# Eight gather buffers instead of four, and the returned rows added in steps of five behind the first late tile's sum

## What is computed

```python
x = x + xattn(layernorm(x), ctx)
h = layernorm(x)
shared_out = expert(h, shared_up[0], shared_down[0])
probs = softmax(h @ router_w)                   # 8 experts
top_k_prob, top_k_idx = top_k(probs, 2)         # two per row
routed_out = sum_e gates[..., e] * expert(h, routed_up[e], routed_down[e])
return shared_out + routed_out + x              # expert: gelu(h @ up) @ down
```

## Time and profile before

| | us |
|---|---|
| median of 3 runs | 2279.95 |
| lowest, highest | 2277.34, 2282.57 |
| the profiled execution, its own time | 2280.16 |
| its span, first to last instruction | 2278.4 |
| outside the span | 1.76 |
| TensorE busy | 2210.9 (97%) |
| VectorE busy | 1804.1 (79%) |

### The profile page before, as it was taken

How to read it: one execution, slowest core, us unless ns; L and a number is a source line. 1 busy time by engine, 2 the same in 40 slices (tenths; PEclk the granted TensorE clock), 3 DMA queues, 4 the chain that set the end, 5 groups by cost and what they waited for, 6 DMA issues and landing times. The chain is left out here.

```text
span 2278.4 us, 40701 instructions
## 1 busy us (share of the span) xinstructions
PE 2210.9 (97%) x13782; PEld 1571.2 (69%) x13782; DVE 1804.1 (79%) x2424; ACT 1370.5 (60%) x2035; POOL 270.1 (12%) x300
## 2 busy tenths in 40 slices
PE   5999999999999999999999999999997999999997
PEld 4656666665666666566566666655886999999996
DVE  6898889899899988989988997898533555557776
ACT  5676566567567666756756765564433555567762
POOL 1100000000001000000000010001472111122210
PEclk8999999999999999999999999999998999999998
DMA  6336236334433522542452362223563434446656
GB/s 238 87 102 187 72 88 185 96 95 126 137 93 105 181 78 84 157 129 75 118 161 85 102 188 78 68 69 123 183 226 121 130 123 136 129 140 218 219 196 225
DMA packets 149277, 305.01 MB, mean 134 GB/s; under 512 B 34784, under 2 KB 71776, under 8 KB 146080
## 3 DMA queue, kind: packets, MB, share of 16 engines
q1 hardware_dynamic: 138688, 272.46, 38.9%
q0 software_dynamic: 10176, 30.45, 3.7%
q10 hardware_dynamic: 288, 0.26, 0.0%
HBM read 189.31 MB, written 79.20 MB: 118 GB/s over the span
## 5 line engine op out<-in xcount | busy, mean ns | idle before, releaser
L927 ACT ACTIVATE probs<-scores 128x1024 f32<-128x1024 f32 x512 | 504.3, 1024 | 212.3 <-PE scores L742 116.4
L1206 DVE TENSOR_TENSOR sums<-sums,probs 128x1024 f32<-128x1024 f32 x384 | 470.4, 1225 | 14.3 <-DVE sums L1206 0.5
L795 PE MATMUL sum_ps<-probs,v_nat 128*64 128x512 f32 x2056 | 469.8, 599 | 1.1 <-DVE probs L1099 1.1
L742 PE MATMUL scores<-q_split,k_split 64*128 64x512 f32 x3072 | 427.2, 409 | 1.6 <-issue 1.5
L1099 DVE TENSOR_SCALAR probs<-probs 128x2048 f32<-128x2048 f32 x256 | 312.9, 1222 | 144.6 <-ACT probs L927 143.9
L742 PEld LDWEIGHTS scores<-q_split,k_split 64*128 64x128 f32 x3072 | 268.9, 185 | 161.1 <-issue 64.1
L1791 PE MATMUL sum_ps<-down,hid_split 128*128 128x256 f32 x2640 | 353.7, 284 | 7.7 <-DVE acc L1934 3.6
L1791 PEld LDWEIGHTS sum_ps<-down,hid_split 128*128 128x128 f32 x2640 | 341.4, 192 | 26.1 <-issue 8.6
L1768 PE MATMUL scores<-xT,up 128*128 128x512 f32 (+1 forms) x1680 | 350.6, 350 | 0.0
L1925 DVE TENSOR_TENSOR hid_split<-hid,hid_split 128x512 fp32r<-128x512 f32 x205 | 142.0, 693 | 227.5 <-ACT hid_split L1855 227.5
L795 PEld LDWEIGHTS sum_ps<-probs,v_nat 128*64 128x64 f32 x2056 | 136.0, 136 | 267.6 <-issue 265.0
(11 more groups left out here) (212 smaller groups left out, 2307.7 us busy)
## 6 DMA issues: line engine op xcount, KB each, us to landing
k_two<-k_two SPq DMA_DIRECT2D x252, 128.0 KB, 2.3
w_all<-wpack SPq DMA_DIRECT2D x60, 512.0 KB, 4.6
raw<-L_ffn_routed_up SPq DMA_DIRECT2D x27, 1024.0 KB, 6.0
raw<-L_ffn_routed_down SPq DMA_DIRECT2D x27, 1024.0 KB, 5.3
rden<-rden_rows SPq DMA_DIRECT2D x128, 128.0 KB, 2.9
ctx_parts<-stage SPq DMA_DIRECT2D x28, 512.0 KB, 5.5
ctx_all<-ctx_parts SPq DMA_DIRECT2D x14, 1024.0 KB, 7.0
sorted_rows<-zero POOLq DMA_DIRECT2D x64, 162.5 KB, 2.9
```

The source lines that it names most:

```text
L742: last = pe.matmul(scores[j % 2][:, head], k_split[i][own, a, j * P:(j + 1) * P], q_split[i][own, m], start=n == 0, stop=n == 2)
L795: last = pe.matmul(sum_ps[64 * head:64 * head + 64, p % 2], v_nat[p // 2 % 2][:, j, cols:cols + 64], probs[:, j % PROBS, head], start=j == ...
L927: act.activation(probs[:, j % PROBS], scores[j % 2][:], ACT.Exp, scale=float(HD) ** -0.5).then_inc(s_exp, 1)
L1206: v.tensor_tensor(to, to, probs[:, j % PROBS], ALU.add).then_inc(s_add, 1)
```

## The change

Three things change. The list `gat` gets four more buffers, the two halves of `up` and of `down` of the last routed tile, so each batch has its own and SP issues all eight loads without a wait between them; the stores follow. The unit of work on VectorE becomes the part: `combine(count)` does the next `count` parts, each of which now increments a semaphore (`s_part_added`). And the distribution is new: 5 parts behind the steps f = 5 to 8 of `late(0)`, none behind f = 9, then `shared_sum`, then 12 parts (`BETWEEN`), then 5 behind each of the steps f = 2 to 6 of `late(1)`, and the remaining 7 behind f = 7. Before it was 4 behind each of f = 6 to 9 and of f = 2 to 7, and 24 more at the end, so 28 in one run.

```diff
-    gat = [t[:, 0:2 * QT * D].rearrange("p (t n d) -> p t n d", n=2, d=D) for t in pair + raw[1 - ROUTED % 2]]
-    GATS = len(gat)
+    gat = [t[:, 0:2 * QT * D] for t in pair + raw[1 - ROUTED % 2]]
+    gat += [t[:, h].bitcast(F32) for t in (up[ROUTED % 2], down[ROUTED % 2]) for h in range(2)]
+    gat = [t.rearrange("p (t n d) -> p t n d", n=2, d=D) for t in gat]
...
         for b in range(B):
-            if b >= GATS:
-                sp.wait_ge(s_half, 2 * (b - GATS + 1))
             src = ys[2 * (b * N + 1):2 * (b * N + N + 1)]
-            sp.dma_start(gat[b % GATS], src.rearrange("(p t n) d -> p t n d", p=P, n=2)).then_inc(s_gat[b % GATS], 16)
-            if b >= GATS:
-                store(b - GATS)
-        for b in range(B - GATS, B):
-            sp.wait_ge(s_half, 2 * (b + 1))
+            sp.dma_start(gat[b], src.rearrange("(p t n) d -> p t n d", p=P, n=2)).then_inc(s_gat[b], 16)
+        for b in range(B):
+            sp.wait_ge(s_part_added, 2 * QT * (b + 1))
...
+        def combine(count):
+            for _ in range(count):
+                b, n, t = added[0] // (2 * QT), added[0] // QT % 2, added[0] % QT
+                if t == 0:
+                    if n == 0:
+                        if b >= HEAD:
+                            v.wait_ge(s_y, late(1).T)
+                        v.wait_ge(s_gat[b], 16)
+                    else:
+                        v.wait_ge(s_part_added, added[0])
                 q = b * QT + t
-                last = v.scalar_tensor_tensor(acc[b][:, t], gat[b % GATS][:, t, n], gate[n][:, q:q + 1], acc[b][:, t], ALU.mult, ALU.add)
-            last.then_inc(s_half, 1)
+                v.scalar_tensor_tensor(acc[b][:, t], gat[b][:, t, n], gate[n][:, q:q + 1], acc[b][:, t],
+                                       ALU.mult, ALU.add).then_inc(s_part_added, 1)
+                added[0] += 1
-        COMBINE = [(0, f) for f in range(6, FT + 2)] + [(1, f) for f in range(2, FT)]
+        PARTS = 2 * QT * B
+        COMBINE = {(0, f): 5 for f in range(5, FT + 1)} | {(1, f): 5 for f in range(2, FT - 1)}
+        BETWEEN = 3 * QT
...
             if t.batch is not None:
                 if n is None:
-                    for half in range(len(COMBINE), 2 * B):
-                        combine(half // 2, half % 2)
-                    v.wait_ge(s_half, 2 * B)
+                    combine(PARTS - added[0])
+                    v.wait_ge(s_part_added, PARTS)
                 shared_sum(t)
+                if is_late(t) and n is not None:
+                    combine(BETWEEN)
```

More of the change, by code:

```diff
@@ L1421, in routing @@
         return ap.rearrange("p (a b) -> p a b", b=shape[1])
-    gat = [t[:, 0:2 * QT * D].rearrange("p (t n d) -> p t n d", n=2, d=D) for t in pair + raw[1 - ROUTED % 2]]
-    GATS = len(gat)
+    gat = [t[:, 0:2 * QT * D] for t in pair + raw[1 - ROUTED % 2]]
+    gat += [t[:, h].bitcast(F32) for t in (up[ROUTED % 2], down[ROUTED % 2]) for h in range(2)]
+    gat = [t.rearrange("p (t n d) -> p t n d", n=2, d=D) for t in gat]
+    assert len(gat) == B
     stage = [t[:] for t in rows] + [t[:, h * QT * DW:(h + 1) * QT * DW].rearrange("p (t d) -> p t d", d=DW)
@@ L1477, in experts @@
     s_back, s_free = sem("f_back"), sem("f_free")
-    s_gat = [sem(f"f_gat{i}") for i in range(GATS)]
-    s_half = sem("f_half")
+    s_gat = [sem(f"f_gat{b}") for b in range(B)]
+    s_part_added = sem("f_part_added")
     s_comb = sem("f_comb")
@@ L2074, in address @@
             v.tensor_tensor(dest[n.u][:, 0:q], whither[:, 0:q], aside[:, 0:q], ALU.add).then_inc(s_dest, 1)
[L2076 to L2084, removed]
-                q = b * QT + t
-                last = v.scalar_tensor_tensor(acc[b][:, t], gat[b % GATS][:, t, n], gate[n][:, q:q + 1], acc[b][:, t], ALU.mult, ALU.add)
-            last.then_inc(s_half, 1)
-        COMBINE = [(0, f) for f in range(6, FT + 2)] + [(1, f) for f in range(2, FT)]
+        added = [0]
+        def combine(count):
[8 more added lines that the diff above has]
+                        v.wait_ge(s_part_added, added[0])
+                q = b * QT + t
+                v.scalar_tensor_tensor(acc[b][:, t], gat[b][:, t, n], gate[n][:, q:q + 1], acc[b][:, t],
[4 more added lines that the diff above has]
+        BETWEEN = 3 * QT
         def body(t, n, m):
@@ L2113, in body @@
                     address(n)
-                if is_late(t) and (t.batch - HEAD, f) in COMBINE:
-                    half = COMBINE.index((t.batch - HEAD, f))
-                    combine(half // 2, half % 2)
+                if is_late(t):
+                    combine(COMBINE.get((t.batch - HEAD, f), 0))
             if t.batch is not None:
                 if n is None:
-                    for half in range(len(COMBINE), 2 * B):
-                        combine(half // 2, half % 2)
-                    v.wait_ge(s_half, 2 * B)
+                    combine(PARTS - added[0])
+                    v.wait_ge(s_part_added, PARTS)
                 shared_sum(t)
+                if is_late(t) and n is not None:
+                    combine(BETWEEN)
         tiles(v, body)
```

## The result

The changed kernel takes 2268.47 us (median of 5 runs, 2267.68 to 2272.21) against 2279.95 before; the ratio is 0.9952, with a 95% interval of 0.9941 to 0.9963, which is 8.4 to 13.5 us. The forecast was 2270.6, 9.4 us less. The profiled execution took 2272.21 with a span of 2270.4.

A forecast was written before the change was run, and what follows sets the result against it. VectorE's chain, not TensorE, was taken to bound the end: parts 17.47, `hidden` 3.66, `shared_sum` 1.13, waits 0.58, together 22.84 us, 9.40 earlier; 2280.16 - 9.40 = 2270.8, less 0.2 for the median, 2270.6; range 2266.8 to 2275.0.

The forecast's parts named there:

- The tail belongs to VectorE, not to TensorE: From `shared_sum` of `late(0)` on, VectorE's list sums to 22.84 us, so the last `shared_sum` starts 9.40 us earlier.
- Five parts fit into a step: In `late(0)`, five parts cost 1.99 to 2.10 us, with a `hidden` 2.6 to 2.7, within TensorE's step of 2.82.
- The border: At `shared_sum` of `late(0)`: sum 1.59 us earlier, TensorE's idle shrinks from 1.97 to 0.38 us, clock stays up.
- The clock is no term of the sum: Behind `shared_sum` of `late(0)`: VectorE's 2.4 us of slack towards ScalarE's last gelu bears a half clock's 1.7 us.
- The loads: Eight loads, served in issue order about 2.45 us apart, land before use: load 5 at 2239.3, load 8 at 2246.6.
- Signals: Each part's increment on VectorE costs nothing; at most 3.6 us if all 44 parts lost their overlap.
- Rival 1: Signals or short waits on VectorE cost more: every part loses its overlap, 3.6 us less gain, 2274.2; chance 0.10.
- Rivals 2, 3 and 4: Loads share with stores, 2275.6, chance 0.07; loads served side by side, 2286, 0.03; clock stays low for long, 2271.6, 0.08.
- The other signs: Wrong if `late(1)` work waits on a load, twelve parts exceed 4.9 us, or sum's end to span's end exceeds 3.7.
- TensorE's last waits: TensorE waits for `hidden` ahead of its last two down products, 0.5 and 1.2 us.
- The size in the medians: Whole kernel: 9.40 us less, 2270.6 us, 0.41% less; chance of faster by over 0.2% is 0.87.

The follow-up runs named there:

- e3: Against the changed kernel: eight buffers kept, parts as before, but the four behind f = 9 moved behind `shared_sum` of `late(0)`; 2276.39 us, ratio 0.9984.
- e4: Against the changed kernel: five of the twelve parts moved back ahead of `shared_sum` of `late(0)`, behind f = 9; 2271.43 us, ratio 0.9962.
- e1: Against the changed kernel: eight buffers and early loads kept, parts back in their old places; 2278.8 us, ratio 0.9995.
- e2: Against the changed kernel: four buffers with late loads as before, parts in the new order; 2270.5 us, ratio 0.9952.
- e8: Against the changed kernel: only the last part of each four increments the semaphore, 16 increments instead of 64; 2270.95 us, ratio 0.9954.
- e9: Against the changed kernel: four GpSimd copies of 128x1024 on idle buffers added, nobody waits for them; 2273.24 us, one execution.
- e6: Against the changed kernel: batch 2's eight parts done by GpSimd, `BETWEEN` 7, four parts at the end; 2274.82 us, ratio 0.9987.
- e10: Against the changed kernel: four GpSimd additions of 128x1024 on idle buffers added, nobody waits for them; 2276.5 us, one execution.
- e5: Against the changed kernel: the twelve parts of `BETWEEN` moved to the very end, 19 instead of 7 behind the last `hidden`; 2272.76 us, ratio 0.9966.
- e11: Against the changed kernel: eight GpSimd memsets of 128x1024 on idle buffers added, nobody waits for them; 2273.94 us, one execution.

## Why the prediction was right

- *The tail belongs to VectorE, not to TensorE.* Right. The sum of 22.84 us for its list measured 22.78, and with the unit prices taken from before: the run of twelve, with one wait for its own part, took 4.88 us (2243.86 to 2248.74), as forecast.
- *Five parts fit into a step.* Right: 2.06 to 2.19 us, and `hidden` kept its rhythm of 2.82 (2230.84, 2233.66). It was close: the later one starts with no idle time shown.
- *The border.* TensorE's idle 0.39, forecast 0.38; the clock stayed up at 1.00, where before it was 0.50 behind the wait of 1.97 and an up product took 2.75 us instead of 1.55. It stayed up in all seven traces with a wait of 0.39 at this place. The comparison with the wait of 1.39 was a fair ground (it left the clock up in all thirteen traces), but length alone doesn't decide: see the last section. e3 gives the worth of both, 3.2 us where 3.3 was expected.
- *The clock is no term of the sum.* Right for this kernel: nothing made VectorE wait behind the border. e4 shows that this rests on VectorE's slack: a longer wait reached the end with 1.30 us (1.4 expected).
- *The loads.* Right in order and near in size. Load 1 landed 4.7 us after its issue, so 1.3 us ahead of its part; the eighth 19.9 after, at 2249.0, 12 us ahead. The first store came behind all loads and took 14.8 us, which nobody waited for. e1 and e2 go beyond the prediction, which had left open whether the buffers are needed: they aren't.
- *Signals.* Free, as taken: 22.78 us between the two sums with 16 signals (e8) as with 64. Rival 1 is out. The parts start 0.397 us apart at 0.478 each, before and after.
- *Rivals 2, 3 and 4* didn't occur: no part waited on a load, the eight loads landed one behind the other, 2.5 to 3.5 us apart (2230.15 to 2248.97), and the clock was 1.00 behind the 0.39.
- *The other signs.* The twelve parts stayed under 4.9 us, no part or `hidden` of `late(1)` waited on a load, and from the last sum's end to the end of the span it is 3.7 us, as before.
- *TensorE's last waits.* 0.20 and 0.88 us of shown idle, forecast 0.5 and 1.2. The forecast counted from start to start; from 2258.26 + 1.43 to 2260.05 it is 0.36, from 2260.05 + 1.43 to 2262.63 it is 1.15. The first was a little smaller.
- *The size in the medians.* 11.5 us against 9.4. The trace puts 9.5 into the tail; the interval of 8.4 to 13.5 holds both. The scatter ahead of the tail is larger than the difference of 2.1, so as far as the runs show it is chance that the medians moved by more than forecast.

## What to carry to other kernels

A share of 97% for TensorE says nothing about the last 2% of the span: list the engine that the final chain runs on, sum up its own work from there, and fill its idle time in earlier steps as far as its slack goes. Work that isn't needed by a sum that another engine waits for belongs behind that sum; a wait at the head of TensorE can cost more than its length when the clock falls with it (1.58 us less of wait gave 3.2 in e3). Where runs scatter by as much as the gain, measure in the trace from a fixed event ahead of the change to the end.

## What the runs showed of the hardware

GpSimd work that reads SBUF isn't free beside a busy VectorE: four additions of 128x1024 on idle buffers lengthened the tail by 8.0 us (47.59 against 39.56), four copies by 2.6 (42.13), eight memsets by nothing (39.54).

A wait at the head of TensorE's list held what stood behind it: in the earlier trace rows no matmul began in the 1.97 us, and the up product behind the held down product started at 2246.00, 1.84 us after it.

At the border TensorE's clock fell within or behind waits of 1.97 us (before and e1), 2.37 (e4), 2.99 (e9), 7.25 (e6) and 7.67 (e10) and stayed up behind 0.39 (seven traces). Elsewhere in the program a wait of 1.39 to 1.40 left it up in all thirteen traces. But the length of a wait alone doesn't decide. A wait of 1.97 us near 1585 stands in all thirteen; the clock fell within it or close behind it in eight and stayed at 1.00 in five (e1, e3, e5, e10, e11). These are the changed kernel and `e3_border_only`:

```profile
1586.52 1.77 PE L1790 MATMUL sum_ps<-down,hid_split 128*128 128x256 f32 x12 [1.97 <-DVE rden L1293]
1588.00:1590.00 2.00, 2.00 (x6) 1.51 (x5) 0.02 (x1) 0.00 (x0) 0.00 (x0) 0.50 0.00 0
```
```profile
1589.12 1.66 PE L1790 MATMUL sum_ps<-down,hid_split 128*128 128x256 f32 x12 [1.97 <-DVE rden L1293]
1591.00:1593.00 2.00, 2.00 (x11) 1.74 (x11) 0.00 (x0) 0.00 (x0) 0.00 (x0) 1.00 0.00 0
```

So a wait of some 2 us puts the clock at risk and doesn't always bring it down; what decides it no run here shows. Whether the kernel before lost the clock at its border in the executions without a trace is open too.
